# First layers of the experts with weights stationary, and weight addresses added ahead of the matmuls

## The chip, the core and the metric

One core of one Trainium2 chip runs the whole program. The metric is the device time of one launch in microseconds (us), from the first to the last instruction and what lies around them. The core has five engines with queues of their own: TensorE (PE) multiplies, VectorE (DVE), ScalarE (ACT) and GpSimd (POOL) do elementwise work, SyncE (SP) issues transfers. They meet only through semaphores. A matmul on PE is two instructions: a weight load, which puts the stationary 128x128 operand into the array (PEld in the profile), and the matmul proper, which streams the moving operand, one column per step.

## The reference

```python
x = x + _layernorm(attn(_layernorm(x)))       # x is 2 x 2048 x 256, one head of 128
x = x + _layernorm(ffn(_layernorm(x)))

def ffn(z):                                    # D = 256, F = 512, 8 experts, top 2
    for _ in range(2):
        z_norm = _rmsnorm(z, norm_w)
        scores = softmax(z_norm @ router_w)
        topk_vals, topk_idx = top_k(scores, 2)
        topk_vals = topk_vals / (sum(topk_vals) + EPS)
        ...
        for e in range(8):
            h = silu(z_norm @ w1[e]) * (z_norm @ w3[e])
            mixed = mixed + cw[:, e] * (h @ w2[e])
        z = z + mixed
    return z
```

The kernel computes only the two chosen experts of each token: it sorts the rows by expert and works on tiles of 128 rows that share one expert.

## The kernel before, in words

Up to about 359 us the kernel does attention for both batch halves, and beside it splits all expert weights into two f16 parts, a high and a low one; both stay in SBUF in `w_all`. A product of two split numbers is three f16 matmuls (high by high, low by high, high by low).

Then come 142 expert tiles in four passes (25, 46, 25 and 46 tiles). Tile `n` holds 128 gathered rows in the buffer `e_xT[u]`, already transposed by DMA, u being n modulo 3. All loops are unrolled; the code is written per engine, and the order on each engine is the order of the code. The semaphores alone join them. For tile `n`:

- PE reads the number of the tile's expert into a register (`expert`, L920). The place of a weight is computed from it.
- `inner` (L930) is the first layer, once for `w1` into the PSUM bank `psum_a` and once for `w3` into `psum_b`: six matmuls each, with 128 rows of `e_xT` stationary and 512 columns of the weight moving. The result has rows on partitions and the 512 features along the bank.
- ACT makes silu of `psum_a` (`silu`, L909). DVE multiplies it with `psum_b` into `h_row` (`gate`, L915).
- PE turns `h_row` by four f32 transposes into the bank `psum_h` (`turn_h`, L2325), so that features stand on partitions.
- ACT takes the f16 high half of the turned rows (`h_hi`, L2082) and DVE the low half (`h_lo`, L2264).
- `outer` (L2336) is the second layer: twelve matmuls with 128x128 parts of `hT` stationary and 256 columns of `w2` moving, into `psum_e`.
- ACT copies the result (`y_copy`, L2089), POOL sends it to DRAM by an indirect DMA (L1980).

PE runs ahead by one tile: the order is `turn_h(n-1)`, `expert(n)`, `inner(n)` twice, then `outer(n-1)`. ACT's order is `h_hi(n-1)`, `silu(n)`, side work, `y_copy(n-1)`; DVE's is `h_lo(n-1)`, `gate(n)`, side work. The side work is the routing of the next pass, sums of results, and transposes and logits (L2300, L764), placed tile by tile by the table `plans`. POOL fetches the rows of tile n+4 (L891) and SP turns those of n+2 (L903).

In the attention stage three kinds of matmul occur that are spoken of later: L1799 (values by probabilities, 128x128 f16 weight, 128 moving columns), L1758 (scores; in the loop its weight is named by a register, and such rows show no shape), and L662 in the routing (a 128x128 f16 weight, 46 columns).

## Time and profile before

| | us |
|---|---|
| median of 3 runs | 1051.33 |
| lowest and highest run | 1049.51, 1053.65 |
| profiled execution | 1050.72 |
| span in that profile | 1049.0 |
| PE, DVE, ACT, POOL busy in the span | 987.4, 690.5, 574.7, 579.5 |

The profiled execution lies 1.7 us above its span, which counts from the first to the last instruction. The granted clock of TensorE is 0.99 to 1.00 of its full level (2.4 GHz) while PE has work, and 0.50 in the last 8 us, when it has none; its mean is 0.989. In all rows L12 is line 12 of the kernel. The end of a matmul in the profile is modelled, and matmuls overlap, so the time that one costs is best read from start to start.

### The profile page before, as it was taken

The numbers are of one execution on the slowest core, as the hardware profiler recorded it, in microseconds if no ns is written. First come the engines' busy times: TensorE is split into PE (matmuls) and PEld (weight loads), VectorE is DVE, ScalarE is ACT, GpSimd is POOL, SyncE is SP. The second block draws the span as 40 slices with busy tenths as digits, with TensorE's granted clock in tenths as the row PEclk, the third lists the DMA queues.
The fourth block names the chain that finished last, engine by engine and source line by source line (L and its number), as shares of the span: only waits on it lengthen the run. The fifth ranks groups of instructions, "written<-read, shape, count | busy, mean of one in ns | idle before, by whom it ended". The sixth has DMA issues, their size and how long they took to land.

```text
span 1049.0 us, 22711 instructions
## 1 busy us (share of the span) xinstructions
PE 987.4 (94%) x7246; PEld 678.7 (65%) x7246; DVE 690.5 (66%) x1497; ACT 574.7 (55%) x1122; POOL 579.5 (55%) x755
## 2 busy tenths in 40 slices
PE   7999997989999899999999999999999999999991
PEld 5677776668888577665666765666755566666661
DVE  7889987999999454684435557535469433575557
ACT  4578786668888545433335565335574333333333
POOL 3356686866798755444443366443365544455435
PEclk9999999999999999999999999999999999999996
DMA  9921111000000234334346435338434433665573
GB/s 315 370 68 31 38 32 22 1 6 21 15 26 16 67 107 125 87 69 101 91 109 167 132 98 139 88 106 181 112 111 117 96 91 92 170 173 119 143 187 130
DMA packets 153818, 109.26 MB, mean 104 GB/s; under 512 B 100992, under 2 KB 140544, under 8 KB 153728
## 3 DMA queue, kind: packets, MB, share of 16 engines
q1 hardware_dynamic: 140096, 70.82, 26.5%
q0 software_dynamic: 13632, 37.24, 12.0%
q8 instruction: 56, 0.92, 0.4%
q14 instruction: 34, 0.28, 0.1%
HBM read 54.27 MB, written 31.20 MB: 81 GB/s over the span
## 4 chain that ended last, share of the span: by engine, by line
PE 69%; DVE 9%; POOL 7%; DMA 6%; ACT 4%; issue 3%; SPq 0%; another core or an unknown queue 0%; POOLq 0%; ACTq 0%; DVEq 0%
PE psum_s L930 32%; PE psum_o L2336 16%; PE psum_s L2325 6%; DMA arena<-arena 4%; PE psum_s L1758 3%; PE psum_t L1753 2%; PE psum_t L764 2%; PE psum_o L1804 2%; POOL arena L1057 2%; DVE arena L1489 1%; DMA arena<-in_rope 1%; PE psum_o L1799 1%; PE psum_o L1811 1%; PE psum_s L1735 1%; PE psum_t L2300 1%
## 5 line engine op out<-in xcount | busy, mean ns | idle before, releaser
L930 PE MATMUL psum_s<-w_all,arena 128*128 x1704 | 392.0, 380 | 4.6 <-issue 1.9
L1980 POOL DMA_INDIRECT token_rows<-arena,result_row_of_row x142 | 147.1, 1036 | 296.5 <-ACT arena L2089 291.2
L930 PEld LDWEIGHTS psum_s<-w_all,arena 128*128 128x128 f16 x1704 | 157.8, 98 | 185.2 <-issue 10.9
L2336 PE MATMUL psum_o<-w_all,arena 128*128 x1704 | 209.4, 273 | 9.1 <-DVE arena L2264 8.2
L915 DVE SCALAR_TENSOR_TENSOR arena<-psum_s,gate_scale,arena 128x512 f32<-128x512 f32 x142 | 106.5, 750 | 161.1 <-ACT arena L909 80.6
L2336 PEld LDWEIGHTS psum_o<-w_all,arena 128*128 128x128 f16 x1704 | 164.7, 98 | 54.1 <-issue 15.4
L2264 DVE TENSOR_TENSOR arena<-psum_s,arena 128x512 f16<-128x512 f32 x142 | 97.8, 689 | 132.3 <-ACT arena L2082 114.2
L2089 ACT ACTIVATE arena<-psum_o 128x256 f32<-128x256 f32 x142 | 54.3, 383 | 216.8 <-PE psum_o L2336 214.1
L891 POOL DMA_INDIRECT arena<-sorted_rows,token_of_row x142 | 139.9, 986 | 49.3 <-issue 40.2
L909 ACT ACTIVATE arena<-psum_s,silu_scale 128x512 f32<-128x512 f32 x142 | 97.6, 687 | 108.1 <-PE psum_s L930 56.6
L2082 ACT ACTIVATE arena<-psum_s 128x512 f16<-128x512 f32 x142 | 84.7, 597 | 33.1 <-PE psum_s L2325 22.9
L2325 PE MATMUL psum_s<-ident,arena 128*128 128x128 f32 x568 | 86.2, 274 | 3.4 <-DVE arena L915 2.6
L1758 PE MATMUL psum_s<-arena 128*128 128x512 f16 x384 | 88.1, 379 | 0.8 <-DVE arena L1498 0.8
L1237 ACT ACTIVATE arena<-psum_s,arena,alpha 128x1024 f32<-128x1024 f32 x64 | 76.5, 1200 | 18.6 <-DVE arena L1528 18.6
L1509 DVE TENSOR_REDUCE arena<-psum_s 128x1 f32<-128x1024 f32 x64 | 76.3, 1216 | 2.5 <-PE psum_s L1758 1.7
L1167 ACT ACTIVATE arena<-psum_t 128x512 f32<-128x512 f32 (+1 forms) x113 | 62.0, 595 | 20.3 <-PE psum_t L1753 19.3
L2325 PEld LDWEIGHTS psum_s<-ident,arena 128*128 128x128 f32 x568 | 67.3, 145 | 6.2 <-DVE arena L915 2.8
L1753 PE MATMUL psum_t<-ident,arena 128*128 128x128 f32 x452 | 60.3, 274 | 5.3 <-ACT arena L1237 3.2
L1758 PEld LDWEIGHTS psum_s<-arena 128*128 (+1 forms) x384 | 37.4, 98 | 39.4 <-DVE arena L1498 1.4
L1753 PEld LDWEIGHTS psum_t<-ident,arena 128*128 128x128 f32 x452 | 51.4, 141 | 12.5 <-ACT arena L1237 3.8
L2123 DVE SCALAR_TENSOR_TENSOR arena<-arena,gates 128x256 f32<-128x256 f32 x128 | 54.4, 487 | 0.1
L1804 PE MATMUL psum_o<-arena 128*128 128x128 f32 x384 | 50.0, 280 | 0.5 <-ACT arena L1167 0.5
(326 smaller groups left out, 1364.8 us busy)
## 6 DMA issues: line engine op xcount, KB each, us to landing
arena<-token_rows SPq DMA_DIRECT2D x64, 256.0 KB, 3.1
w_all<-in_L_ffn_w SPq DMA_DIRECT2D x24, 512.0 KB, 10.1
sorted_rows<-w_all SPq DMA_DIRECT2D x24, 256.0 KB
out<-x_sb SPq DMA_DIRECT2D x7, 512.0 KB, 3.1
arena<-arena SPq DMA_TRANSPOSE x172, 2.4
arena<-sorted_rows,token_of_row POOLq DMA_INDIRECT x142
token_rows<-arena,result_row_of_row POOLq DMA_INDIRECT x142
x_sb<-in_L_attn_x SPq DMA_DIRECT2D x1, 2048.0 KB, 14.8
```

Source lines behind the costliest of these rows:

```text
L891: nc.gpsimd.indirect_dma_start(x_pair[:, u, :, :].rearrange("p l d -> p (l d)"), None, rows, bass.IndirectOffsetOnAxis(ap=sources[:, at : ...
L909: nc.scalar.activation(silu_a, psum_a, ACT.Silu, scale=silu_scale[:, 0:1]).then_inc(s_silu, 1)
L915: nc.vector.scalar_tensor_tensor(h_row, psum_b, gate_scale[:, 0:1], silu_a, ALU.mult, ALU.mult).then_inc(s_h, 1)
L930: last = nc.tensor.matmul(bank, e_xT[:, u, lx * DC + c, :], w_split[:, bass.ds(e * EW + at, FF)], start=(q == 0), stop=(q == 3 * DC - 1))
L1237: nc.scalar.activation(probs[:, h * S // 2 : (h + 1) * S // 2], psum_s[:, h * S // 2 : (h + 1) * S // 2], ACT.Exp, bias=neg_max, scale=alp ...
L1753: last = nc.tensor.transpose(psum_t[g % 2][:, k * P : (k + 1) * P], probs[:, kc * P : (kc + 1) * P], ident[:, :])
L1758: last = nc.tensor.matmul(psum_s[:, kb * 512 : (kb + 1) * 512], qkT[:, lq, 0, bass.ds(i * P, P)], qkT[:, lk, 1, kb * 512 : (kb + 1) * 512] ...
L1980: nc.gpsimd.indirect_dma_start(rows, bass.IndirectOffsetOnAxis(ap=targets[:, at : at + 1], axis=0), y_row[:, u, :], None).then_inc(s_sent[ ...
L2082: nc.scalar.activation(hT[:, 0, :, :].rearrange("p c t -> p (c t)"), psum_h, ACT.Copy).then_inc(s_h_hi, 1)
L2264: nc.vector.tensor_tensor(hT[:, 1, :, :].rearrange("p c t -> p (c t)"), psum_h, hT[:, 0, :, :].rearrange("p c t -> p (c t)"), ALU.subtract ...
L2325: last = nc.tensor.transpose(psum_h[:, c * P : (c + 1) * P], h_row[:, c * P : (c + 1) * P], ident[:, :])
L2336: last = nc.tensor.matmul(psum_e, hT[:, lh, c, :], w_split[:, bass.ds(e * EW + at, D)], start=(q == 0), stop=(q == 3 * FC - 1))
```

## The change

The first layer swaps its operands. A 128x128 block of the weight is now stationary and the 128 columns of `e_xT` move, four blocks of features after each other in one bank, six matmuls each: 48 per tile instead of 12, and the result has features on partitions already. So `turn_h` with its four transposes, its bank and its semaphore go. `gate` writes `h_all` in that layout, and `h_hi` and `h_lo` read it from SBUF where they read PSUM.

The first layer gets new waits, since nothing else now orders PE behind the readers of its banks: the `w1` half of tile `n` waits for silu of tile n-1, the `w3` half for the gate of tile n-1. The gate waits for the low half of the tile before.

The addresses: before, each matmul's place was worked out by register instructions just ahead of it. Now `place` adds the byte address straight into a register, all of a layer's places ahead of the layer, and the matmuls name the registers (`stationary`, `moving`). A stationary operand is named by its last column.

```diff
+        W_BASE, LAST_COLUMN = 16512, 2 * (P - 1)
...
-        h_row = take(FF)
+        h_all = take(FF)
...
             dve.wait_ge(s_b, s + 1)
             dve.wait_ge(s_silu, s + 1)
-            nc.vector.scalar_tensor_tensor(h_row, psum_b, gate_scale[:, 0:1], silu_a, ALU.mult,
+            if s:
+                dve.wait_ge(s_h_lo, s)
+            nc.vector.scalar_tensor_tensor(h_all, psum_b, gate_scale[:, 0:1], silu_a, ALU.mult,
                                            ALU.mult).then_inc(s_h, 1)
...
+        def place(pe, e, at):
+            r = pe.alloc_register()
+            pe.reg_alu(r, e * (2 * EW), 2 * at + W_BASE, ALU.add)
+            return pe.snap(r, donate=True, min_val=2 * at + W_BASE, max_val=2 * at + W_BASE + 2 * EW * (NE - 1),
+                           guaranteed_mod_val=0, out_of_modulus=2)
+
+        def stationary(r):
+            return w_bytes[:, bass.ds(r - (W_BASE + LAST_COLUMN), 2 * P)].bitcast(F16)
+
+        def moving(r):
+            return w_bytes[:, bass.ds(r - W_BASE, 2 * D)].bitcast(F16)
+
         def inner(pe, n, e, m):
             u = n % UNROLL
+            places = [[place(pe, e, ((m * DC + c) * 2 + lw) * GROUP + f * P + P - 1) for c in range(DC) for lw in range(2)] for f in range(FC)]
             if m == 0:
                 pe.wait_ge(s_turned[u], 16 * (n // UNROLL + 1))
+                if n:
+                    pe.wait_ge(s_silu, n)
+            elif n:
+                pe.wait_ge(s_h, n)
             bank, signal = ((psum_a, s_a), (psum_b, s_b))[m]
-            for q, (c, lx, lw) in enumerate([(c, a, w) for c in range(DC) for a, w in ((0, 0), (1, 0), (0, 1))]):
-                at = ((m * DC + c) * 2 + lw) * GROUP
-                last = nc.tensor.matmul(bank, e_xT[:, u, lx * DC + c, :], w_split[:, bass.ds(e * EW + at, FF)],
-                                        start=(q == 0), stop=(q == 3 * DC - 1))
+            for f in range(FC):
+                for q, (c, lx, lw) in enumerate([(c, a, w) for c in range(DC) for a, w in ((0, 0), (1, 0), (0, 1))]):
+                    last = nc.tensor.matmul(bank[:, f * P : (f + 1) * P], stationary(places[f][2 * c + lw]),
+                                            e_xT[:, u, lx * DC + c, :], start=(q == 0), stop=(q == 3 * DC - 1))
             last.then_inc(signal, 1)
...
             def h_hi(s):
-                act.wait_ge(s_th, s + 1)
-                nc.scalar.activation(hT[:, 0, :, :].rearrange("p c t -> p (c t)"), psum_h, ACT.Copy).then_inc(s_h_hi, 1)
+                act.wait_ge(s_h, s + 1)
+                nc.scalar.activation(hT[:, 0, :, :].rearrange("p c t -> p (c t)"), h_all, ACT.Copy).then_inc(s_h_hi, 1)
...
-            def turn_h(n):
-
-                pe.wait_ge(s_h, n + 1)
-                for c in range(FC):
-                    last = nc.tensor.transpose(psum_h[:, c * P : (c + 1) * P], h_row[:, c * P : (c + 1) * P], ident[:, :])
-                last.then_inc(s_th, 1)
-
             def outer(n, e):
+                per = GROUP // D
+                places = [[place(pe, e, ((2 * DC + c // per) * 2 + lw) * GROUP + c % per * D) for lw in range(2)] for c in range(FC)]
                 pe.wait_ge(s_h_lo, n + 1)
                 if n:
                     pe.wait_ge(s_yrow, n)
...
                     n = FIRST[k] + t
-                    if n:
-                        turn_h(n - 1)
                     e = expert(pe, k, t)
```

On PE, one expert tile of the second pass stood like this before. ISA is a register instruction of several steps (three for an address), `x2` two equal rows, and the names in brackets the semaphores waited for; the first layer is L930, the second L2336, and the pattern of address and matmuls goes on between the rows shown.

```order
L2325 MATMUL psum_s<-ident,arena 128x128 [waits h_ready]
L2325 MATMUL psum_s<-ident,arena 128x128 x3
L920 TENSOR_LOAD expert_of
L920 ISA x2
L930 ISA [waits x_rows_turned1]
L930 MATMUL psum_s<-w_all,arena 128x512 x2
L930 ISA
L930 MATMUL psum_s<-w_all,arena 128x512
L930 ISA
L930 MATMUL psum_s<-w_all,arena 128x512 x2
```

The same place on PE now, one whole tile from the number of the expert to the second layer (L2348) of the tile before it:

```order
L922 TENSOR_LOAD expert_of
L922 ISA x2
L926 ISA x3
L949 MATMUL psum_s<-arena,w_all 128x128 [waits silu_ready,x_rows_turned2]
L949 MATMUL psum_s<-arena,w_all 128x128 x23
L926 ISA x3
L949 MATMUL psum_s<-arena,w_all 128x128 [waits h_ready]
L949 MATMUL psum_s<-arena,w_all 128x128 x23
L926 ISA x2
L2348 MATMUL psum_o<-w_all,arena 128x256 [waits y_row_ready,hT_lo]
L2348 MATMUL psum_o<-w_all,arena 128x256 x11
```

The transposes and their wait for the gate are gone, that wait stands ahead of the second half of the next first layer, sixteen register instructions per tile have become eight of up to six steps, and they stand ahead of the layers rather than in them.

On ACT the order before, from silu of one tile to silu of the next:

```order
L909 ACTIVATE arena<-psum_s,silu_scale 128x512 [waits a_ready]
L2089 ACTIVATE arena<-psum_o 128x256 [waits y_row_sent0,expert_out_ready]
L2082 ACTIVATE arena<-psum_s 128x512 [waits h_turned]
L909 ACTIVATE arena<-psum_s,silu_scale 128x512 [waits a_ready]
```

and now:

```order
L909 ACTIVATE arena<-psum_s,silu_scale 128x512 [waits a_ready]
L2108 ACTIVATE arena<-psum_o 128x256 [waits y_row_sent0,expert_out_ready]
L2101 ACTIVATE arena<-arena 128x512 [waits h_ready]
L909 ACTIVATE arena<-psum_s,silu_scale 128x512 [waits a_ready]
```

The order is kept; the high half (L2101) waits for the gate itself and reads SBUF.

## Rows read from the trace of the kernel before

**Rows 1.** The page: busy time by engine, and the chain that ended last by engine.
```profile
PE 987.4 (94%) x7246; PEld 678.7 (65%) x7246; DVE 690.5 (66%) x1497; ACT 574.7 (55%) x1122; POOL 579.5 (55%) x755
...
PE 69%; DVE 9%; POOL 7%; DMA 6%; ACT 4%; issue 3%; SPq 0%; another core or an unknown queue 0%; POOLq 0%; ACTq 0%; DVEq 0%
```

**Rows 2.** Windows: length, busy us by engine, granted clock, DMA share, GB/s.
```profile
359.30:1031.00 671.70, 654.00 (x4344) 421.56 (x4344) 366.75 (x803) 304.63 (x604) 325.59 (x325) 1.00 0.47 119
...
608.00:662.00 54.00, 49.78 (x313) 30.24 (x311) 35.59 (x95) 33.48 (x68) 35.21 (x40) 1.00 0.44 120
...
761.00:812.00 51.00, 46.23 (x318) 28.46 (x317) 42.26 (x101) 31.86 (x65) 32.89 (x36) 1.00 0.43 115
```

**Rows 3.** Timeline of PE, a plain tile: start, length, engine, line, what.
```profile
488.62 1.47 PE L2336 MATMUL psum_o<-w_all,arena 128*128 x12
489.93 0.60 PE L2325 MATMUL psum_s<-ident,arena 128*128 128x128 f32 x4
490.38 2.76 PE L930 MATMUL psum_s<-w_all,arena 128*128 x12
492.98 1.47 PE L2336 MATMUL psum_o<-w_all,arena 128*128 x12
```

**Rows 4.** Timeline of PE in the attention stage.
```profile
306.26 1.50 PE L1799 MATMUL psum_o<-arena 128*128 128x128 f16 x24
```

**Rows 5.** Groups by line and shape: count, then busy us and mean ns of one.
```profile
L1799 PE MATMUL psum_o<-arena 128*128 128x128 f16 x588 | 38.0, 219 | 0.0
...
L1799 PEld LDWEIGHTS psum_o<-arena 128*128 128x128 f16 x588 | 35.5, 98 | 0.7
L1758 PEld LDWEIGHTS psum_s<-arena 128*128 x276 | 27.0, 98 | 27.4
```

**Rows 6.** Timeline of PE, 24 short matmuls and what follows them.
```profile
464.74 0.77 PE L662 MATMUL psum_t<-arena 128*128 128x46 f16 x24
465.35 0.92 PE L2336 MATMUL psum_o<-w_all,arena 128*128 x7
```

**Rows 7.** The first layer's line: its register instructions, ns least, median, most.
```profile
L930 PEldq FUSED_REGOPS  x1136: 46/46/51, 350.6 to 1021.0; - x190
```

**Rows 8.** Timeline of DVE and ACT in the tile of rows 3.
```profile
488.82 0.75 DVE L915 SCALAR_TENSOR_TENSOR arena<-psum_s,gate_scale,arena 128x512 f32<-128x512 f32 x1 [1.29 <-ACT arena L909]
...
490.13 0.38 ACT L2089 ACTIVATE arena<-psum_o 128x256 f32<-128x256 f32 x1 [1.92 <-PE psum_o L2336]
...
490.56 0.60 ACT L2082 ACTIVATE arena<-psum_s 128x512 f16<-128x512 f32 x1
...
491.19 0.69 DVE L2264 TENSOR_TENSOR arena<-psum_s,arena 128x512 f16<-128x512 f32 x1 [0.98 <-ACT arena L2082]
```

**Rows 9.** Groups by line and shape: forms of ACT and DVE that read SBUF.
```profile
L1174 ACT ACTIVATE arena<-arena 128x512 f16<-128x512 f32 x15 | 9.3, 622 | 0.0
...
L2147 DVE TENSOR_TENSOR x_sb<-x_sb,arena 128x256 f32<-128x256 f32 x16 | 6.0, 418 | 0.0
```

**Rows 10.** Timeline of PE in a routing stretch; in brackets idle time and what ended it.
```profile
642.93 1.54 PE L2336 MATMUL psum_o<-w_all,arena 128*128 x12 [1.66 <-DVE arena L2264]
```

**Rows 11.** Timeline of the last pass: the low half and its use.
```profile
1013.02 0.66 DVE L2264 TENSOR_TENSOR arena<-psum_s,arena 128x512 f16<-128x512 f32 x1
...
1014.06 1.47 PE L2336 MATMUL psum_o<-w_all,arena 128*128 x12
```

**Rows 12.** Waits: who waited for whom, us in total, times, longest.
```profile
ACT arena L909 <- remote: 4.8, 2, 2.4
...
PE psum_s L2325 <- DVE arena L915: 2.6, 4, 1.0
...
PE psum_s L930 <- issue: 1.9, 7, 0.4
```

**Rows 13.** Timeline of PE behind one late silu.
```profile
476.35 0.63 PE L2325 MATMUL psum_s<-ident,arena 128*128 128x128 f32 x4 [0.83 <-issue]
...
477.31 2.76 PE L930 MATMUL psum_s<-w_all,arena 128*128 x12 [0.33 <-issue]
```

More of the change, by code:

```diff
@@ L2356, in _ @@
                     before_e = e
-            turn_h(ALL - 1)
             outer(ALL - 1, before_e)
```

9 lines of the change are left out of this document (3 added, 6 removed).

## The prediction

> **What bounds the kernel now.** I read the page first. TensorE (PE) is busy 94% of the span and holds 69% of the chain of work that ended last [rows 1]. A busy share alone does not say which stage a change touches, so the second view is the table of windows. From 359.3 to 1031 us, where the 142 expert tiles run, PE is busy 654.0 of 671.7 us, against 367 for VectorE (DVE), 305 for ScalarE (ACT) and 326 for GpSimd, at the full granted clock [rows 2]. Only 17.7 us are idle there. The third view is PE's timeline of one tile without side work [rows 3]. Taking starts only, one tile is 4.36 us: 12 second-layer matmuls (L2336) 1.31, four transposes (L2325) 0.45, 12 first-layer matmuls (L930) 2.60, and nothing between them. This stage is a queue of PE work with no holes, so time taken off PE there comes off the span until another engine is late.
>
> **What goes.** The four transposes, 0.45 us of PE per tile [rows 3], all on the path: 142 x 0.45 = 63.9 us. With them goes the link gate, transpose, high half; ACT now reads the gate's result directly.
>
> **What the first layer costs now.** The same columns stream, but as 48 matmuls of 128 columns instead of 12 of 512, each with a weight load of its own. The price of one is its pace, start to start, not its mean duration. Before: 2.60/12 = 0.217 us for 512 columns [rows 3]. For 128 columns of f16 with a new 128x128 weight each time the attention stage has the row: L1799, 24 in 1.50 us [rows 4], with 0.219 the length of one [rows 5], so (1.50 - 0.219)/23 = 0.0557 us. Then 48 x 0.0557 = 2.67 us against 2.60: 0.07 us more per tile. I take a tile of 1.31 + 2.67 = 3.98 to 3.99 us, 0.37 less than 4.36. That is 142 x 0.37 = 52.5 us.
>
> **Does that pace hold with weights named by a register?** Three rows bear on it. Weight loads of 98 ns are hidden behind matmuls at a pace of 56 ns, so two are under way at once [rows 4, 5]. A weight load named by a register (L1758 in its loop) has the same 98 ns [rows 5], but stands beside 512 columns. And the queue hands out pairs of load and matmul faster than needed: L662, with 46 columns, starts 24 in 465.35 - 464.74 = 0.61 us, 26 ns each [rows 6]. No row shows a register-named operand at a pace under L2336's 1.31/12 = 109 ns [rows 3]. So the bounds are 26 ns of dispatch below (then the columns bind, 56 ns, the value I take, since L1799 is the same load and the same columns) and 98 ns above, each load finished before the next. Nothing excludes the upper end but L1799. The tile breaks even at (4.36 - 1.31)/48 = 63.5 ns.
>
> The Trainium skill ("TensorE: Matmul & The Clock Gate", section "Back-to-back issue gap") speaks against this change: in streams of load and matmul it gives about 81 ns at 128 columns and about 131 ns at 512. By these figures the first layer would go from 12 x 131 = 1.57 to 48 x 81 = 3.89 us, an estimate of +1.9 us per tile after the transposes are gone, some 265 us in all. The trace has 56 and 217 ns instead [rows 3, 4], and it decides.
>
> **The addresses.** Before, a register instruction of 46 ns stands ahead of every matmul or pair of them, 8 per layer and 16 per tile [rows 7]; now 8 per tile stand in groups of 3, 3 and 2 ahead of the layers, each with up to six additions. PE's own row shows they are hidden today [rows 3]. After: reading the expert's number and making the first eight or so addresses stands between the last second-layer matmul dispatched and the first of the next tile. The queue covers it with those 12 matmuls still to run, 1.31 us; today much of the work is covered by the four transposes, 0.45 us, with no gap. Dispatch of a tile: 60 pairs x 26 ns = 1.56 us plus 8 x 46 ns, under 2 us, plus the number read, under 3.99. I cost it at nothing; if the cover fails, at most the 0.44 us that the transposes stood for is exposed.
>
> **The chain of the gated rows.** From the trace of a plain tile [rows 8]: gate at 488.82 (0.75), y copy on ACT at 490.13, high half at 490.56, low half on DVE 491.19 to 491.88, used at 492.98. The second layer starts at 488.62 and 492.98 [rows 3]. Now the high half follows the y copy, which is before it in ACT's order and ends at 490.51, so it gains only 0.05 us, though the gate is long done. The low half is ready 3.2 us after the second layer's start and needed 3.98 after it: 0.8 us of slack where 1.1 is today. Both halves now read SBUF rather than PSUM. ACT's row for that form is 622 ns against 0.60 us [rows 8, 9]. DVE has no such form in SBUF at 512 columns; a 256-wide add there takes 418 ns [rows 9], so between 0.69 as from PSUM and twice 418, 0.84; I keep 0.69, since a fixed part is in both. Either end lies inside the slack. The added PE waits (first bank for silu, second for the gate) look back one tile: silu and gate end about 1 us into the second layer, before PE returns to those banks. Behind a waiting PE stand all later matmuls.
>
> **Where the gain is lost or added.** (a) In the routing stretches DVE binds: at 642.93 PE has idled 1.66 us for the low half (L2264) [rows 10]; 608 to 662 and 761 to 812 hold 9.0 of the 17.7 idle us [rows 2]. Counting tiles whose DVE work is 4 us or more, or that end in such a wait, I get 14. A shorter PE gains nothing there: -14 x 0.37 = -5.2. (b) The tiles with long but not binding DVE work: the low half of 1013.02 (0.66) ends 0.38 before its use at 1014.06 [rows 11], as much as the tile shortens; about 15 such tiles at 0.1: -1.5. (c) Today PE stops at the transposes when the gate is late. The waits on the gate itself are 2.6 us; twice silu waited on "remote", 4.8 us in all [rows 12], and in one of these places PE idled 0.83 and 0.33 at the transposes and behind them [rows 13]. Now PE needs only silu at that point, and the gate half a first layer (1.3 us) later: +3.5, most of these. (d) 60 pairs instead of 28 per tile are more code. What the profile lays on "issue" before L930 is 1.9 us [rows 12]; between nothing and once more that much, and I take -1.5, since the code doubles.
>
> **Sum.** 52.5 - 5.2 - 1.5 + 3.5 - 1.5 = 47.8 us. The profiled execution took 1050.7 (span 1049.0): 1002.9. It lies 0.6 under the median of 1051.3, so **1004 us**. The attention stage and the end after the last tile only shift.
>
> **Rivals.** (1) *The boundary is exposed.* The sequencer, not PE, sets the time between tiles, since its waits, the read of the expert's number and three long register instructions follow each other. For it: "issue" already ends some idle time before L930 [rows 12]. Against: 1.31 us of cover, and no gap in [rows 3]. Half of 0.44 us exposed per tile: 142 x 0.22 = 31, so 1035 us; all of it would end at 1066. (2) *Short matmuls do not hold 56 ns* (slower). Weight loads of register-named places are not hidden behind only 128 columns. Place: L949, all 142 tiles; it decides from 63.5 ns. At 70 ns: 142 x 48 x 14.3 ns = 97 more than my sum, 1101 us; at the upper bound of 98: 142 x 48 x 42 = 288 more, 1292 us. Only L1799 speaks against it. The skill's figure of 81 ns, beside the measured 216 for before, would be this rival: an estimate of 1176. (3) *DVE binds more widely*: if the low half takes the 0.84 of the upper bound and DVE's side work meets it, some 40 tiles lose their 0.37: +15, so 1019 us. For it: the 0.38 us in [rows 11]. Against: DVE is busy 367 of 671.7 us [rows 2]. (4) *Nothing changes*, since another engine sets the tile: 1051; excluded almost wholly by 654 busy of 671.7.
>
> **How the numbers follow.** Forecast with its small terms off by up to 10 us: 0.68. Rival 3: 0.09. Rival 1: 0.11 in all, of it 0.02 with no gain and 0.01 slower. Rival 2: 0.10. Rival 4: 0.02. Low end: 52.5 plus the 3.5 and half of the other idle time, about 58 off: 993, with a little for (a) counted too high, 994. The high end takes in rival 3 and most of rival 1: 1032. The rest above is about 0.15, below 0.03. A difference of 0.5% is about what a measurement of this kernel can tell from none. Faster by more: 0.68 + 0.09 + 0.08 of rival 1 = 0.85; within: rival 4 and 0.02 of rival 1, 0.04; slower: 0.11.
>
> **What the changed profile would show.** Right: L949 groups of 48 in 2.67 + 0.2 us, mean 219 ns, plain tiles at 3.99, no transposes, PE idle mostly before L2348 for DVE. Rival 1: idle time on "issue" before L949 in every tile. Rival 2: groups of L949 longer than 3.05 us. Rival 3: L2283 above 0.8 us and waits for it outside the routing stretches. I am wrong if a plain tile is over 4.1 us, or if the idle time on DVE grows past 25 us.

## The result, and the profile after

The changed kernel took 1036.16 us (median of 4 runs, 1034.16 to 1038.62) beside 1052.28 for the kernel before: a ratio of 0.985, 95% interval 0.982 to 0.988. The forecast was 1004 us and the range 994 to 1032, so the sign was right, the gain was 16 us where 48 was expected, and the time lies outside the range. One thing has to be said ahead of the rows: repeated later, the same kernel took 1011.5, 1007.7 and 1035.4 us on different occasions, each time beside the kernel before on the same chip. It has two levels, and the experiments below are about what goes with each of them. The first profile belongs to the 1036 level.

Its page, busy time by engine and the chain (answers to [rows 1]):

```profile
span 1034.0 us, 30800 instructions
...
PE 946.7 (92%) x11790; PEld 837.9 (81%) x11790; DVE 692.9 (67%) x1497; ACT 568.7 (55%) x1122; POOL 591.0 (57%) x755
...
PE 61%; DVE 13%; POOL 8%; issue 5%; ACT 5%; DMA 5%; another core or an unknown queue 2%; ACTq 0%; POOLq 0%; SPq 0%; DVEq 0%
```

PE on a plain tile and the start of the next (answers to [rows 3]):

```profile
484.59 1.47 PE L2348 MATMUL psum_o<-w_all,arena 128*128 x12
485.90 2.84 PE L949 MATMUL psum_s<-arena,w_all 128*128 128x128 f16 x48
488.58 0.49 PE L2348 MATMUL psum_o<-w_all,arena 128*128 x3
```

488.58 - 484.59 = 3.99 us where it was 4.36. The 48 short matmuls take 2.68 from start to start, 56 ns each, and nothing stands between the layers. Below is the stretch in which the tiles run, from the first second-layer matmul to the start of the second layer of the last tile but one: first of the kernel before, then of the changed one. The columns are length, busy us (count) of PE, PEld, DVE, ACT and POOL, granted clock, DMA share, GB/s.

```profile
359.33:1022.90 663.57, 650.65 (x4317) 418.96 (x4318) 360.41 (x784) 301.19 (x597) 320.55 (x316) 1.00 0.47 120
```

```profile
359.92:1007.70 647.78, 610.12 (x8797) 575.25 (x8798) 362.89 (x784) 295.22 (x597) 331.42 (x317) 1.00 0.51 124
```

PE is busy 40.5 us less, yet the stretch is only 15.8 us shorter: PE's idle time in it went from 12.9 to 37.7 us. So most of the work taken off PE came back as waiting. Who waits for whom in the tiles (us in total, times, longest; answers to [rows 12]):

```profile
DVE arena L917 <- PE psum_s L949: 148.5, 95, 2.4
ACT arena L909 <- PE psum_s L949: 101.6, 118, 2.9
...
ACT arena L909 <- remote: 23.7, 8, 4.4
PE psum_o L2348 <- DVE arena L2283: 22.3, 17, 2.6
DVE arena L917 <- remote: 15.0, 5, 4.4
```

PE waits for the low half 22.3 us (8.2 before), and the consumers of PE wait for something that the profile can only call "remote", its word for a wait that it can lay on no instruction (4.8 us before, now 23.7 and 15.0). The timeline of all engines in the plain tile shows what is odd:

```profile
483.81 0.94 PE L949 MATMUL psum_s<-arena,w_all 128*128 128x128 f16 x14
484.07 0.97 POOL L891 DMA_INDIRECT arena<-sorted_rows,token_of_row  x1 [0.30 <-issue]
484.59 1.47 PE L2348 MATMUL psum_o<-w_all,arena 128*128 x12
485.70 0.75 DVE L917 SCALAR_TENSOR_TENSOR arena<-psum_s,gate_scale,arena 128x512 f32<-128x512 f32 x1 [1.87 <-PE psum_s L949]
485.74 1.19 SPq L903 DMA_TRANSPOSE arena<-arena  x1
```

The last first-layer matmul ends at 483.81 + 0.94 = 484.75. The gate on DVE waits for nothing else (it has idled 1.87 us), and starts at 485.70, 0.95 us late. In the kernel before it starts 0.04 us after its matmul [rows 3, 8]. SP, which waits for the same signal, is as late (485.74). I call a start **late** if ScalarE's silu or VectorE's gate is free, has its other input, and still begins over 0.1 us after the end of the matmul that signals it. Counted over 141 tiles from the traces: before 5 silus and 6 gates (5.7 us in sum), changed kernel 55 silus and 102 gates (138 us). A **held signal** is the cause named by the trace: its own event of the semaphore comes that late too (over 0.1 us in counts by window, over 0.3 in the table below; signals without a recorded event are left out).

Held signals have a pattern. Of the first-layer signals whose matmul ended 0.2 to 1.1 us after the start of a gather issue of GpSimd (L891), 100 of 105 were held in the changed kernel. Of the 107 that were over 0.3 us late and whose matmul ended at most 1.5 us after a gather's start, 93 were released 1.4 to 1.9 us after that start. In the kernel before, 2 of 40 in the same window were held. That is a part only, since 132 of its 284 first-layer signals have no event in the trace; by the readers, which all have rows, 3 of 100 signals in the window were late before and 100 of 107 in the changed kernel.

The "remote" waits are the same thing. The 8 of silu and the 5 of the gate are just the signals that came over 1.5 us after their matmul. The longest stand where GpSimd issues several gathers in a row:

```profile
470.66 0.97 POOL L891 DMA_INDIRECT arena<-sorted_rows,token_of_row  x1 [0.30 <-issue]
471.93 0.95 POOL L891 DMA_INDIRECT arena<-sorted_rows,token_of_row  x1 [0.30 <-issue]
473.71 0.51 PE L949 MATMUL psum_s<-arena,w_all 128*128 128x128 f16 x6 [0.98 <-issue]
473.74 0.75 DVE L917 SCALAR_TENSOR_TENSOR arena<-psum_s,gate_scale,arena 128x512 f32<-128x512 f32 x1 [4.35 <-remote]
```

The gate's matmul ended at 470.05, and its signal came 3.66 us later, 1.8 us after the start of the last gather. PE itself stopped as well, in the middle of a first layer and with no wait in its code there, and went on at the same moment. Five such stops of 0.5 to 1.0 us ended 1.75 to 1.80 us after a gather's start. So a hold is mostly, but not only, one of signals.

### The profile page after: what moved, and what is told of

Read it like the earlier page. It is cut to its first block, busy times and chain, and to the rows that moved or that the text cites. A ratio compares the mean times of both kernels' runs of the same rounds, so it can differ in the third digit from the quotient of the medians.

```text
span 1034.0 us, 30800 instructions
## 1 busy us (share of the span) xinstructions
PE 946.7 (92%) x11790; PEld 837.9 (81%) x11790; DVE 692.9 (67%) x1497; ACT 568.7 (55%) x1122; POOL 591.0 (57%) x755
## 3 DMA queue, kind: packets, MB, share of 16 engines
q0 software_dynamic: 13632, 37.24, 12.8%
## 4 chain that ended last, share of the span: by engine, by line
PE 61%; DVE 13%; POOL 8%; issue 5%; ACT 5%; DMA 5%; another core or an unknown queue 2%; ACTq 0%; POOLq 0%; SPq 0%; DVEq 0%
PE psum_s L949 31%; PE psum_o L2348 15%; DMA arena<-arena 4%; PE psum_s L1777 3%; PE psum_t L1772 2%; PE psum_t L766 2%; PE psum_o L1823 2%; POOL arena L1076 2%; DVE arena L1508 1%; DVE arena L2283 1%; PE psum_o L1818 1%; PE psum_s L1754 1%; PE psum_o L1830 1%; DVE arena L917 1%
## 5 line engine op out<-in xcount | busy, mean ns | idle before, releaser
L949 PE MATMUL psum_s<-arena,w_all 128*128 128x128 f16 x6816 | 407.0, 219 | 13.2 <-issue 7.2
L949 PEld LDWEIGHTS psum_s<-arena,w_all 128*128 x6816 | 390.7, 98 | 23.1 <-issue 16.8
L1999 POOL DMA_INDIRECT token_rows<-arena,result_row_of_row x142 | 150.2, 1058 | 270.5 <-ACT arena L2108 266.1
L2348 PE MATMUL psum_o<-w_all,arena 128*128 x1704 | 210.7, 273 | 26.9 <-DVE arena L2283 22.3
L2348 PEld LDWEIGHTS psum_o<-w_all,arena 128*128 128x128 f16 x1704 | 160.8, 98 | 49.1 <-DVE arena L2283 25.7
L891 POOL DMA_INDIRECT arena<-sorted_rows,token_of_row x142 | 144.2, 1015 | 48.6 <-issue 41.0
L2283 DVE TENSOR_TENSOR arena<-arena 128x512 f16<-128x512 f32 x142 | 102.3, 720 | 45.3 <-ACT arena L2101 32.5
L2101 ACT ACTIVATE arena<-arena 128x512 f16<-128x512 f32 x142 | 88.9, 626 | 4.6 <-DVE arena L917 2.3
L1823 PEld LDWEIGHTS psum_o<-arena 128*128 128x128 f32 x384 | 45.4, 192 | 1.0 <-ACT arena L1186 0.8
L1523 DVE SCALAR_TENSOR_TENSOR arena<-psum_t,arena 128x512 f16<-128x512 f32 x49 | 32.2, 687 | 10.6 <-ACT arena L1186 9.7
```

The lines of the kernel that those rows point to most:

```text
L891: nc.gpsimd.indirect_dma_start(x_pair[:, u, :, :].rearrange("p l d -> p (l d)"), None, rows, bass.IndirectOffsetOnAxis(ap=sources[:, at : ...
L949: last = nc.tensor.matmul(bank[:, f * P : (f + 1) * P], stationary(places[f][2 * c + lw]), e_xT[:, u, lx * DC + c, :], start=(q == 0), sto ...
L1823: last = nc.tensor.matmul(psum_o[:, 0:P], v_whole[:, kc, :], pT_whole[:, (kc - HALVED) * P : (kc - HALVED + 1) * P], start=False, stop=(kc ...
L1999: nc.gpsimd.indirect_dma_start(rows, bass.IndirectOffsetOnAxis(ap=targets[:, at : at + 1], axis=0), y_row[:, u, :], None).then_inc(s_sent[ ...
L2101: nc.scalar.activation(hT[:, 0, :, :].rearrange("p c t -> p (c t)"), h_all, ACT.Copy).then_inc(s_h_hi, 1)
L2283: nc.vector.tensor_tensor(hT[:, 1, :, :].rearrange("p c t -> p (c t)"), h_all, hT[:, 0, :, :].rearrange("p c t -> p (c t)"), ALU.subtract) ...
```

## Experiments

Each set of runs shares a chip and the kernel before. "Held" counts signals of PE, of all its lines, more than 0.3 us late; the first profile of the kernel before has 10.

| set | before, us | kernels: us (ratio), held |
|---|---|---|
| first | 1052.3 | changed 1036.2 (0.985), 148 |
| 1 | 1051.2 | e1 1050.2 (0.999), 10; e2 1267.1 (1.205), 115; e3 1019.4 (0.969), 48; e4 1041.0 (0.989), 162 |
| 2 | 1051.5 | e5 1019.1 (0.971), 73; e6 1050.5 (0.999), 8; e7 1123.5 (1.071), 133 |
| 3 | 1048.9 | e8 1011.5 (0.963), 0; e9 1008.0 (0.960), 0 |
| 4 | 1048.7 | e12 1011.5 (0.963), 0; e13 1010.9 (0.964), 0; e10 1009.5 (0.964), 0; e11 1062.9 (1.014), 0 |
| 5 | 1048.6 | e14 1007.7 (0.962), 0; e15 1061.4 (1.012), 0; e16 1009.7 (0.964), 0 |
| 6 | 1051.3 | e17 1035.4 (0.985), 136; e18 1019.9 (0.971), 44 |

### e1 and e2: the two halves of the change

e1 has only the register places:

```
+            places = [[place(pe, e, ((m * DC + c) * 2 + lw) * GROUP) for lw in range(2)] for c in range(DC)]
...
-                last = nc.tensor.matmul(bank, e_xT[...], w_split[:, bass.ds(e * EW + at, FF)],
+                last = nc.tensor.matmul(bank, e_xT[...], moving_row(places[c][lw]),
```

> The kernel before with the places of the weights added into registers (14 register instructions ahead of each stretch of matmuls instead of one ahead of each matmul), and nothing else: rows stay stationary, weights move, the gated rows are still transposed. A matmul of 512 columns takes 216 ns against 46 ns of register work, so every theory expects no gain: 1050 to 1053 us. What it tells apart is the late signals of the changed kernel (the gate starts 0.9 to 1.2 us after the last first-layer matmul in about 100 tiles, 0.04 us in the kernel before). If the register instructions make them late, the gate is late here too, in most tiles; if the short matmuls or the GpSimd gather's place do, it starts on time here.

1050.15 us, ratio 0.9989 (0.9976 to 1.0001), 4 silus and 6 gates late. The register places alone give nothing that can be told from noise, and hardly more starts are late than before (5 and 6).

e2 has only the stationary weights, with an address worked out ahead of each matmul or pair (the two lines of `places` go, and each loop works out `at`; its first-layer lines):

```
-    last = nc.tensor.matmul(bank[:, f * P : (f + 1) * P], stationary(places[f][2 * c + lw]),
+    last = nc.tensor.matmul(bank[:, f * P : (f + 1) * P], w_split[:, bass.ds(e * EW + (at - LAST_COLUMN // 2), P)],
```

> The changed kernel with the addresses worked out ahead of each matmul, as in the kernel before: weights stationary, no transposes, 60 register instructions a tile where there were 18. If one costs the sequencer 46 ns beside its dispatch, a 56 ns matmul is no longer covered and a tile goes from 3.99 to about 6 us, the kernel to 1250 to 1400 us; if the register work is hidden behind the queue, 1036 us as the changed kernel. Signals: a theory that makes the expert-number load and the block of register instructions late-maker expects the gate on time (no block, queue empty); the theory of the gather expects it late wherever a gather issue runs.

1267.11 us. The first-layer line's register instructions and matmuls (ns least, median, most), and PE on one tile:

```profile
L949 PE MATMUL psum_s<-arena,w_all x6816: 216/227/314, 349.8 to 1237.5; 128*128 128x128 f16 x195
L949 PEldq FUSED_REGOPS  x4544: 46/46/51, 349.7 to 1237.4; - x198
```

```profile
599.82 3.08 PE L949 MATMUL psum_s<-arena,w_all 128*128 128x128 f16 x34
602.90 1.48 PE L2348 MATMUL psum_o<-w_all,arena 128*128 x12
```

34 matmuls in 3.08 us are (3.08 - 0.22)/33 = 87 ns each instead of 56: two register instructions for three matmuls make the sequencer the bound. Their 46 ns are not the whole price: 3 x 26 ns of dispatch [rows 6] and 2 x 46 would be 57 ns per matmul. In the tile shown a weight load starts 49 to 50 ns after a register instruction has ended, so each one takes about 95 ns of the queue. So the register places are what makes the swap pay, and 1267 us is what the expectation named for work that is not hidden. Here 111 silus were late and only 3 gates; with the longer tile the gather falls on the other signal. They fit one rule closely: a signal due 0.4 us after the gather's start was 1.0 to 1.1 us late, one due 0.7 us after it 0.8 us. It comes 1.5 us after the gather's start, whenever it is due. The sequencer does no block of register work here, so neither that block nor a full queue is needed for a hold.

### e3 and e4: gather or sequencer

e3 adds one wait on GpSimd; e4 moves the read of the next expert's number between the two first-layer halves.

```
+                        if n + AHEAD < ALL:
+                            pool.wait_ge(s_b, n + 1)
                         fetch(pool, n + AHEAD)
```

```
-                    e = expert(pe, k, t)
+                    e = ahead_e if t else expert(pe, k, t)
                     for m in range(2 if n else 0):
+                        if m and t + 1 < PASS[k]:
+                            ahead_e = expert(pe, k, t + 1)
                         inner(pe, n, e, m)
...
```

> The changed kernel with one wait added on GpSimd: the gather of the rows four tiles ahead is issued only after the signal of the second first-layer half of the current tile. In the changed kernel 87 of 98 first-layer signals whose matmul ended 0.4 to 0.9 us after such a gather issue began came 0.6 to 1.5 us late, against a few of the others. Theory gather: signals are late while GpSimd issues the gather; here they come on time, the gate starts 0.04 us after the last matmul, and the tiles with logits and routing get back 0.2 to 0.4 us each: 1024 to 1032 us. Theory sequencer (the signal waits while PE's sequencer loads the expert number and does its register block): lateness as before, 1035 to 1038 us. Theory that lateness costs nothing: 1035 to 1038 us with or without late signals.

> The changed kernel with the expert number of the next tile read between the two first-layer halves of a tile instead of at the next tile's start, nothing else moved. Theory sequencer: the second half's signal comes on time in the plain tiles, the first half's may be late instead; time moves by several us, 1028 to 1034 us if the gate is what the routing tiles wait for. Theory gather: lateness as in the changed kernel, 1035 to 1038 us.

e3: 1019.4 us, late gates 102 to 24 (87 to 12 us in sum), late silus 55 to 38. It fell below the expected 1024 to 1032. e4: 1041.0, somewhat above the 1035 to 1038 of the gather theory, gates 96 late, silus 72. Moving the read of the expert's number left the late starts as they were, so the sequencer theory is out; a wait added on GpSimd made the kernel 17 us faster. In e3 the gate is on time and the gather starts behind it:

```profile
479.34 1.47 PE L2350 MATMUL psum_o<-w_all,arena 128*128 x12
479.54 0.75 DVE L917 SCALAR_TENSOR_TENSOR arena<-psum_s,gate_scale,arena 128x512 f32<-128x512 f32 x1 [1.06 <-PE psum_s L949]
479.77 0.97 POOL L891 DMA_INDIRECT arena<-sorted_rows,token_of_row  x1 [1.26 <-PE psum_s L949]
```

These lines are of e18, the same kernel in the last set.

### e5: the scatter too

```
                     if n:
+                        if n + 1 < ALL:
+                            pool.wait_ge(s_a, n + 2)
                         send(n - 1)
```

> The kernel of e3_gather_after_signal (1019.4 us) with a second wait on GpSimd: the scatter of a tile's outputs is issued only after the signal of the first first-layer half of the next tile. In e3 38 silu starts were still late, 29 us in sum, and 43 of the 48 late signals had the scatter as GpSimd's last issue. Theory of the issue (any indirect issue of GpSimd holds back the signal of a first-layer half that ends 0.2 to 1.1 us after its start): silu late in under 10 tiles, 1012 to 1018 us, the tiles with logits at 5.24 us. Rival: the scatter does not hold signals (its own window had 31 late of 101), late starts stay and time is 1018 to 1022 us; and if delaying the scatter makes later rows wait, it is over 1022 us.

1019.1 us, no better than e3. Late silus fell to 17, but 133 gates became late by a third of a microsecond each (48 us in sum): the scatter now starts just behind the first half's signal, and the second half's is due some 1.0 us after its start, inside the window. 120 of 129 first-layer signals in the scatter's window were held. So the scatter can hold as the gather does, and this place for it was badly chosen. It does not always: in the changed kernel 31 of 98 signals in its window were held, and in e3 31 of 101. The expected 1012 to 1018 was wrong for that reason.

### e6: the control

> The kernel before with the same wait on GpSimd ahead of its gathers as e3_gather_after_signal has, a control. If the 17 us that this wait gave the changed kernel came from its late signals, it gives nothing here, where 136 of 141 signals are on time: 1050 to 1053 us. If the gather's place helps for another reason (transfers that collide, the GpSimd queue), this kernel gains too, by 5 to 17 us.

The edit of e3 in the kernel before: 1050.5 us, ratio 0.9989 (0.9979 to 0.9999). The gather's place is worth 1 us, at most 2.2, where hardly any signals are held (8), and this in a set in which short matmuls do get theirs held.

### e7, e11, e15: short matmuls alone

The kernel before with its operands, each first-layer matmul cut into four of 128 columns.

```
+            for f in range(FC):
...
+                    last = nc.tensor.matmul(bank[:, f * P : (f + 1) * P], e_xT[:, u, lx * DC + c, :],
+                                            moving_row(places[c][lw]), start=(q == 0), stop=(q == 3 * DC - 1))
```

> The kernel before with each first-layer matmul of 512 columns cut into four of 128, rows still stationary and weights still moving, gated rows still transposed, places in registers: as many and as short first-layer matmuls as in the changed kernel (48 a tile), with the operands of the kernel before. At 56 ns each a tile costs what it does before, so 1050 to 1056 us if signals are on time. Theory short matmuls: signals that end while GpSimd issues a gather are late here as well, in 40 tiles or more, and the routing and logits tiles grow, 1054 to 1070 us. Theory stationary weights (it is loading the weights from the large weight buffer that makes them late): at most 10 late signals, 1050 to 1054 us.

1123.5 us, ratio 1.071, far over all that was expected. 118 silus and 98 gates are late, and of the first-layer signals in the gather's window 52 of 58. So it is not the stationary weights: with the operands of the kernel before, short matmuls get their signals held too. Here PE itself waits for the gate, at the transposes, and the cost can be seen. GpSimd, ScalarE, PE and DVE on one tile:

```profile
895.21 0.97 POOL L893 DMA_INDIRECT arena<-sorted_rows,token_of_row  x1 [0.30 <-issue]
896.71 0.69 ACT L911 ACTIVATE arena<-psum_s,silu_scale 128x512 f32<-128x512 f32 x1 [2.08 <-PE psum_s L945]
896.97 1.47 PE L2351 MATMUL psum_o<-w_all,arena 128*128 x12
...
897.50 0.75 DVE L917 SCALAR_TENSOR_TENSOR arena<-psum_s,gate_scale,arena 128x512 f32<-128x512 f32 x1 [2.14 <-ACT arena L911]
898.31 0.66 PE L2340 MATMUL psum_s<-ident,arena 128*128 128x128 f32 x4
...
899.36 1.34 PE L945 MATMUL psum_s<-w_all,arena 128*128 x21 [0.39 <-issue]
```

Silu starts 1.50 us after the gather, some 0.9 us behind its matmul, and the gate 0.53 us after the second layer began where it could have started 0.20 after it. The gate ends at 898.25. Behind the wait for it on PE's queue stand the transposes and then the read of the next expert's number, and its row shows that it starts only then (its first start is 898.3, 571 ns):

```profile
L922 PEldq TENSOR_LOAD <-expert_of x1: 571/571/571, 898.3 to 898.3; - x1
```

So the first layer starts 1.05 us after the transposes, which need 0.45, and the tile takes 5.1 us; the same tile takes 4.5 in e15. Of such a delay the profile shows only a part as idle (0.39 of the 0.60 us), since the row of the last transpose reaches on.

Later, where nothing was held, the same kernel (e15) and the one with the gather behind the signal (e11) ran at the same level:

> The kernel of e7_rows_stationary_in_quarters (1123.5 us; rows stationary, first-layer matmuls of 128 columns, 118 silu starts late) with the gather issued only after the second first-layer signal. If late signals alone made e7 slow, 1050 to 1075 us with at most 50 late; if the short matmuls cost time in another way, over 1100 us.

> The kernel of e7_rows_stationary_in_quarters (short first-layer matmuls, rows stationary; 1123.5 us with held signals). Where signals are held: 1115 to 1130 us again. Where none is: within 0.3% of e11's 1063 us, since its wait on the gather then has nothing to avoid; what stays above the kernel before is what the cut itself costs.

1062.9 and 1061.4 us. PE on another tile, of e15, where the gate started 0.20 us after the second layer:

```profile
819.80 1.67 PE L945 MATMUL psum_s<-w_all,arena 128*128 x27
821.31 1.48 PE L2351 MATMUL psum_o<-w_all,arena 128*128 x12
822.62 0.60 PE L2340 MATMUL psum_s<-ident,arena 128*128 128x128 f32 x4
823.10 2.07 PE L945 MATMUL psum_s<-w_all,arena 128*128 x34
```

The first layer starts 0.48 us after the transposes. The cut itself costs 12.8 us (1061.4 against 1048.6), 0.09 us per tile; the held signals cost this kernel 62 more. e11 was expected to show a wait at work; in its set there was nothing to avoid, so it says only that.

### e8 and e9: both issues between two signals; a lighter tile for ScalarE

e8, then a part of e9 (its other edits move the copies' partners on the other engines by the same tile):

```
-                    if n:
-                        send(n - 1)
+                    if n > 1 and t != 1:
+                        send(n - 2)
+                    if n and (t == 0 or n == ALL - 1):
+                        send(n - 1)
```

```
-                if 0 <= t - plan.split - 1 < PAIRS:
-                    row_hi(k, t - plan.split - 1)
+                if 0 <= t - plan.split - 1 - (k > 0) < PAIRS:
+                    row_hi(k, t - plan.split - 1 - (k > 0))
```

> The kernel of e3_gather_after_signal (1019.4 us) with each scatter one tile later, so that GpSimd issues the scatter of tile n-2 right behind the gather, both right after the signal of the second first-layer half; no wait is added. In e5 the scatter sat right after the first half's signal and held the second half's back 0.35 us in 133 tiles. Here both issues run while PE works at the outer layer and the start of the next first layer, 0 to 2 us after one signal and 0.6 us or more before the next. Theory of the issue: silu and gate late in under 15 tiles each, 1012 to 1018 us. Rival: what is left of e3's late signals is not worth time, or the two issues in a row hold the next tile's first half (a hold lasts to 1.5 us after the issue's start, that is to 2.55 us, against its signal at 2.65 us): 1018 to 1024 us.

> The kernel of e3_gather_after_signal with the row splits of the middle two passes (four ScalarE copies of 0.49 us a tile) begun one tile later, so that the tile with the two table loads and the softmax exponentials no longer has them too. In e3 that tile takes 6.26 us (4.49 before) and the one of the third pass 6.83 (5.39 before); the output copy starts 2.5 us after its matmuls there and the outer layer waits 2.05 us. Theory ScalarE (its work in these tiles is longer than the shortened tile): 2 to 4 us back in these tiles, 1015 to 1018 us. Rival (the copies are needed in time by the next pass, or the tile they move into overflows instead): 1019 to 1022 us.

1011.5 and 1008.0 us, both below what was expected, and at first sight two successes. But in neither trace was a single signal held, not even in e9, which keeps e3's places for gather and scatter: 0 of 106 first-layer signals in the scatter's window, where e3 had 31 of 101. Something other than the kernel had changed, and the kernel before ran 2.6 us faster than in the set before it. These two runs could not be compared with e3's. What the late splits do can still be read from the tiles of the later sets without held signals. The ten tiles in which the rows are first split (51 to 60) took 48.0, 47.3 and 46.4 us with the edit (e9, e10, e16) and 48.7, 50.5 and 50.0 without it (e12, e13, e14). The second such stretch (82 to 92) gives nothing: 55.5, 55.8 and 57.2 against 56.7, 55.1 and 55.0. Both together are 103.1 to 103.6 against 105.0 to 105.5, some 2 us, the low end of what the ScalarE theory expected. In the whole time it does not show: e10 and e16 are no faster than the changed kernel beside them, and e9's ratio (0.960, 0.958 to 0.963) and e13's (0.964, 0.963 to 0.966) come from different sets.

### e12, e13, e10: the changed kernel again

> The changed kernel itself, unaltered, beside the three below on one chip. The signals that came late in three jobs (148 later than 0.3 us in the changed kernel, 48 and 73 in e3 and e5) were absent, 0 of 284, in the last one (e8, e9), whose chip was another. Theory placement (e8 and e9 moved the issues out of the way): late signals here again, over 100, and 1033 to 1039 us. Theory chip (how far signals are held depends on the chip, not on the kernel): if this job's chip holds none, the time is 1013 to 1022 us with no late start; if it holds them, as before.

> The kernel of e3_gather_after_signal on the same chip as e12. Theory placement: 1017 to 1021 us and some 40 late signals whatever the chip. Theory chip: on a chip that holds none its time lies within 0.3% of e12's, since the wait then has nothing to avoid; on one that holds them it is 15 to 19 us under e12.

> The kernel of e3 with both later edits: scatters one tile later (e8) and row splits one tile later (e9). Each alone ran at 0.963 and 0.960 of the kernel before, against 0.969 of e3 in another job. If the two act apart, 0.953 to 0.958 of before, 1002 to 1008 us; if e9's gain was the chip's, 0.960 to 0.966, 1010 to 1016 us.

The unaltered changed kernel: 1011.5 us, ratio 0.963 (0.961 to 0.966), no held signal. e13, with the wait that had been worth 17 us: 1010.9, the same. e10: 1009.5, also the same, so its two moves bring nothing that whole times can measure. The same engines, the same stretch as above, in e12:

```profile
360.23:983.23 623.00, 603.50 (x8796) 575.96 (x8797) 367.02 (x784) 290.92 (x597) 328.05 (x317) 0.99 0.52 129
```

24.8 us shorter than in the first profile, with PE idle 19.5 us instead of 37.7. The waits in it:

```profile
DVE arena L917 <- PE psum_s L949: 144.8, 123, 2.4
DVE arena L2283 <- ACT arena L2101: 94.2, 94, 1.9
ACT arena L909 <- PE psum_s L949: 88.6, 135, 1.8
...
PE psum_o L2348 <- DVE arena L2283: 17.4, 16, 2.6
```

"Remote" is gone. And the plain tile, with the gather at the same place in the tile as in the first profile:

```profile
475.20 0.97 POOL L891 DMA_INDIRECT arena<-sorted_rows,token_of_row  x1 [0.30 <-issue]
475.73 1.47 PE L2348 MATMUL psum_o<-w_all,arena 128*128 x12
475.93 0.75 DVE L917 SCALAR_TENSOR_TENSOR arena<-psum_s,gate_scale,arena 128x512 f32<-128x512 f32 x1 [1.05 <-PE psum_s L949]
```

The gate starts 0.04 us after its matmul, 0.73 us after the gather's start. In this window 0 of 98 signals were held. PE's stops are gone too: its idle time on "issue" ahead of the two layers (L949, L2348) is 0.2 us, against 7.2 and 4.2 in the first profile.

### e14, e16, e17, e18: does it come back?

> The changed kernel a third time, unaltered, to see whether the state with held signals comes back: it ran at 1036 us (0.985 of before) with 148 signals later than 0.3 us, and at 1011.5 us (0.963) with none. Theory of two states of the chip or its machine: one of the two, 1033 to 1039 us with over 100 late or 1008 to 1014 us with none, and nothing between; the kernel before 1051 to 1052 us in the first, 1048 to 1049 us in the second. Rival (a sliding effect): a time between, with some tens late.

> The kernel of e10_both_moves (gather behind the second signal, scatter right behind the gather, row splits one tile later). Where signals are held, theory of the issues: both issues stand between two signals, so late starts fall under 30 and the time is 1008 to 1018 us, some 20 us under the changed kernel beside it. Where none is held: as e10, 1008 to 1012 us, no different from the changed kernel.

> The changed kernel a fourth time, beside e18, in a new job, to catch the state with held signals once more. With it: 1033 to 1039 us, over 100 late signals, and the kernel before at 1051 to 1052 us. Without it: 1007 to 1013 us, none, before at 1048 to 1049 us. Nothing between under the theory of two states.

> The kernel of e3 (gather behind the second signal) beside e17. In the state with held signals 15 to 19 us under e17 (1017 to 1021 us); without it within 0.3% of e17.

e14 and e16: 1007.7 and 1009.7 us, none held. e17 and e18, one set later: 1035.4 and 1019.9 us, 136 and 44 held, and in e17 95 of 103 in the gather's window. So there are two conditions and nothing between in the four sets that have the changed kernel, and the pair e17 and e18 stands in one of them on one chip: ratios to before 0.985 (0.981 to 0.989) and 0.971 (0.966 to 0.975), 15.5 us apart. Sets 1, 2 and 6, with held signals, ran on chips 7, 4 and 11, sets 3, 4 and 5, without, on 3, 7 and 13, as the runs number them; the first set has no number on record. The number 7 stands in both, so a chip's number does not decide. What does stays open.

## Why the prediction was right or wrong

**Price of the first layer, the transposes, the addresses: right.** A plain tile is 3.99 us, with 56 ns per short matmul, register-named weights and no gap at the boundary. Rival 2, the Trainium skill's 81 ns ("TensorE: Matmul & The Clock Gate", section "Back-to-back issue gap"), and rival 1 did not happen. e1 and e2 add that the swap needs the register places: without them the pace is 87 ns. The eight register instructions of a tile took 74 ns each (median), not the 46 taken, and were hidden all the same.

**The step that failed: "The chain of the gated rows".** It took the gate's start from one row, 0.04 us after the last first-layer matmul, as if it were fixed, and put the delay of a signal at nothing without a reason; the first profile has 55 silus and 102 gates late, 138 us in sum. The 0.8 us of slack and the sum both rest on it. In plain tiles the slack carried it: the gate comes 0.95 us late and ends at 486.45, but the y copy, which the high half follows in any case, ends at 486.48; the low half is ready in time, and the tile is 3.99 in both conditions. In tiles with more work it did not. From the starts of the second layers, in us:

| tiles | before | changed, held | changed, none held (e12) |
|---|---|---|---|
| 3 to 10, logits of the first pass | 44.7 | 44.3 | 41.5 |
| 11 to 20, routing | 46.8 | 48.1 | 43.8 |
| 43 to 50 and 74 to 81, logits | 89.0 | 91.9 | 85.5 |
| 51 to 60, routing, rows split | 49.8 | 52.0 | 48.7 |
| 82 to 92, routing, rows split | 55.3 | 57.6 | 56.7 |
| 113 to 139, last pass | 117.9 | 112.9 | 109.4 |

A logits tile shows the path. In the first profile silu comes 0.80 us late, and ScalarE's squares and copies, which the logits on PE wait for, follow it; in e12 it is on time:

```profile
566.30 0.97 POOL L891 DMA_INDIRECT arena<-sorted_rows,token_of_row  x1 [0.30 <-issue]
567.72 0.69 ACT L909 ACTIVATE arena<-psum_s,silu_scale 128x512 f32<-128x512 f32 x1 [2.63 <-PE psum_s L949]
568.09 0.61 PE L2319 MATMUL psum_t<-ident,arena 128*128 128x128 f32 x4
```

```profile
556.70 0.97 POOL L891 DMA_INDIRECT arena<-sorted_rows,token_of_row  x1 [0.30 <-issue]
557.12 0.69 ACT L909 ACTIVATE arena<-psum_s,silu_scale 128x512 f32<-128x512 f32 x1 [1.47 <-PE psum_s L949]
...
558.25 0.61 PE L2319 MATMUL psum_t<-ident,arena 128*128 128x128 f32 x4
```

Silu starts 0.37 us before the transposes of the normalised rows in the one, 1.13 us before them in the other. On the medians the changed kernel is 24 to 28 us slower in the condition with held signals (1036.2 and 1035.4 against 1011.5 and 1007.7), e3 9 (1019.4 and 1019.9 against 1010.9), e7 62. The kernel before is slower by 2.6 (1051.3 against 1048.7); it has no trace from a set without, so that its 11 late starts are the reason is not shown. In the stretch of tiles PE idles 18 us more in the first profile than in e12: 4 more on the low half (19.6 against 15.7), 11 more on "issue". Of these 11, 3 are the low half again (it ended 0.06 us before), and 5 are stops of PE in the middle of a layer. Holds are dear where short matmuls end inside an issue's window and a reader, or PE itself, is near the path.

**Term (c) was misread.** The "remote" waits of [rows 12 and 13] were priced as waits that the new kernel would win back, +3.5 us. They were two held signals of the kernel before, 1.7 us late each, and a warning: with short matmuls they became 23.7 and 15.0 us. In the condition without held signals there are none.

**The other terms, by e12 and e14.** Without held signals the gain is 37.2 us (1048.7 - 1011.5) and 40.9 (1048.6 - 1007.7) against 47.8. The 76 tiles that took about 4.35 us and have no side work on PE went from 331.1 to 307.3 us in e12, 0.31 each and not 0.37; term (b) covers that and was too small, since in the last pass 8 of 28 tiles stay at 4.1 to 4.3. The 21 tiles with 12 matmuls of side work gained 0.29 each (118.2 to 112.2). Term (a) was too good: tiles 51 to 60 and 82 to 92 together went from 105.1 to 105.4 us in e12 and 105.0 in e14, so 21 tiles gained nothing where it counted 14. Term (d), more code, has no effect in e12 (first layer's idle time on "issue" 0.2 us); the 7.2 us of the first profile go with the condition, since the code is the same. The low half reads SBUF in 715 to 720 ns against 689 from PSUM, near the value taken, so rival 3 did not happen; neither sign of being wrong was reached, on DVE's waits (22.3 us, the sign was 25) or on the plain tile (3.99, the sign was 4.1): both looked past the place where it failed.

**The range.** It holds the 1007.7 and 1011.5 of the later sets but not the 1036.2 and 1035.4. The forecast knew nothing of the two conditions, so which of them a measurement met was chance. Its upper part was made of rivals 1 and 3, which are about PE's boundary and DVE's speed; delay between two engines was in none of them.

## What to carry to other kernels

When a change makes matmuls shorter, look at the time from the end of a signalling matmul to the start of its reader, in both traces and over all tiles; a reader that idles on PE while PE has long moved on is the sign. If signals are held, keep the start of GpSimd's indirect issues out of the microsecond ahead of them, by one wait on the signal: here that was worth 15 to 17 us where signals were held, and cost nothing where none were. And a result that looks like a success on one chip is to be set beside the kernel it is compared with on that same chip: e8 and e9 would have been credited with 8 to 11 us that were not theirs.

## What the runs showed of the hardware

- The increment of a semaphore by a matmul can come 0.3 to 1.5 us after the matmul's end, mostly while PE goes on at full pace. It happened to first-layer matmuls of 128 columns (56 ns apart in the changed kernel and e7, 87 in e2) that ended 0.2 to 1.1 us after GpSimd began to issue an indirect gather (100 of 105) or, less regularly, a scatter (31 of 98; 120 of 129 in e5). Such an issue lasts 0.97 to 1.06 us, and release was mostly 1.4 to 1.9 us after a gather's start, later where another issue followed (the longest 3.7 us after the matmul). In the gather's window first-layer matmuls of 512 columns were held 2 times in 40, and second-layer ones of 256 columns 3 in 13 in the changed kernel and 2 in 58 in e3.
- Short is not yet the reason. The four f32 transposes of e7 have 128 columns too, but stand 109 ns apart, and 0 of 35 of their signals were held in the scatter's window, where 15 of 19 of its first-layer signals were. Whether the columns, the pace or the number of matmuls ahead of the signal decides was not tried.
- The Trainium skill ("Perfetto Trace Analysis", section "Per-engine timelines") puts the push and the propagation of a matmul's semaphore update behind the end that the profiler reports for it. The traces agree: the matmul's row ends on time, and the delay shows in the semaphore's event and as the reader's idle time.
- This held in four sets of runs and was wholly absent in three (0 of 98 against 100 of 105 for one and the same kernel). The profiles of e12 and of the changed kernel differ by at most 4 us in the summed rows of any line (the first layer's 6816 matmuls), apart from the waits. Neither the mechanism between GpSimd and PE nor what switches it on was found. The issue and the transfers that it starts were never taken apart, and a kernel whose GpSimd issues nothing at all was not tried.
- Register work between short matmuls is not free: two instructions with rows of 46 ns for three matmuls gave 87 ns per matmul, against 56 where the same places stood in registers.
